# The opening of a graph-count build written in another order, with a first group of 256 nodes and keys turned two pairs ahead

## The reference, cut to what matters

```
edge_index = jnp.stack([src, dst])
h = jnp.maximum(_layernorm(x, axis=-1), 0.0)
x = x + _L0_gnn_ref(h, edge_index, ...)
h = jnp.maximum(_layernorm(x, axis=-1), 0.0)
x = x + _L1_gnn_ref(h, edge_index, ...)
```

## Time and profile before

| what | value |
|---|---|
| median of 3 runs | 963.67 us (963.1 to 963.69) |
| the profiled execution's own time | 960.25 us |
| its span | 958.0 us |
| end of `build` on PE | 398.04 us |
| PE busy | 883.7 us |
| DVE busy | 716.7 us |
| ACT busy | 496.7 us |
| POOL busy | 345.8 us |

### The profile page before, as it was taken

The page is one execution under the profiler, slowest core; times in us unless marked ns, Lnnn a source line. Parts: engine busy times, 40 slices in busy tenths (PEclk is TensorE's granted clock), DMA queues, the critical chain, the costliest instruction groups (busy, mean ns, idle before and its releaser), DMA issues.

```text
span 958.0 us, 25402 instructions
## 1 busy us (share of the span) xinstructions
PE 883.7 (92%) x11397; PEld 740.0 (77%) x11397; DVE 716.7 (75%) x679; ACT 496.7 (52%) x534; POOL 345.8 (36%) x255
## 2 busy tenths in 40 slices
PE   0589999999999979989999999999999989999995
PEld 0368888889989969867888887778888867777774
DVE  6879999999999979295667656665656566777672
ACT  2655555464645534264443454443444467777772
POOL 5775674638471640112567645471000000000000
PEclk9999999999999989999999999999999999999998
DMA  3024334433443333415333434434342357777761
GB/s 108 18 80 148 109 120 145 149 126 102 145 149 129 107 117 111 139 40 154 117 115 116 121 111 118 131 116 129 105 116 75 114 174 238 240 238 242 255 196 38
DMA packets 81377, 126.87 MB, mean 132 GB/s; under 512 B 9808, under 2 KB 58064, under 8 KB 81136
## 3 DMA queue, kind: packets, MB, share of 16 engines
q1 hardware_dynamic: 78128, 121.98, 40.8%
q0 software_dynamic: 3136, 3.22, 1.5%
HBM read 84.22 MB, written 40.94 MB: 131 GB/s over the span
## 4 chain that ended last, share of the span: by engine, by line
PE 50%; DVE 5%; issue 2%; ACT 1%; POOL 0%; DVEq 0%; ACTq 0%
PE net_ps_hi L1164 14%; PE net_ps_hi L1147 13%; PE net_ps_lo L1147 13%; PE net_ps_mt L1090 5%; PE net_ps_ft L1090 3%; DVE hT L849 1%; DVE hT L844 1%; PE net_ps_mt L1199 1%; ACT net_wide L1002 1%; DVE net_wide L752 1%; DVE net_first L856 1%; PE net_ps_mt L1194 1%; DVE net_h_parts L920 0%; DVE hT L909 0%; POOL net_wide L798 0%
## 5 line engine op out<-in xcount | busy, mean ns | idle before, releaser
L1002 ACT ACTIVATE net_wide<-net_raw 128x3584 fp32r<-128x3584 uint8 (+1 forms) x77 | 232.6, 3020 | 37.3 <-PE net_ps_hi L1164 25.5
L752 DVE CAST net_wide<-net_raw 128x3584 fp32r<-128x3584 uint8 (+1 forms) x103 | 202.7, 1974 | 65.2 <-PE net_ps_lo L1147 45.1
L1147 PE MATMUL net_ps_hi<-net_wide,net_first 128*128 128x512 f32 (+1 forms) x637 | 248.2, 393 | 0.1
L461 ACT ACTIVATE build_cnts<-build_ps_cnt 128x980 uint16<-128x980 f32 (+4 forms) x176 | 154.3, 901 | 167.1 <-PE build_ps_cnt L551 161.9
L1147 PE MATMUL net_ps_lo<-net_wide,net_first 128*128 128x512 f32 (+1 forms) x637 | 240.6, 381 | 0.0
L571 PE MATMUL build_ps_out<-build_parts_pad,build_cnts 128*128 128x195 bf16 x2401 | 225.4, 250 | 1.0 <-issue 0.9
L342 DVE TENSOR_TENSOR build_hot_lo<-build_grid_lo,build_keys_t 128x4096 bf16<-128x4096 bf16 x100 | 224.6, 2284 | 0.0
L571 PEld LDWEIGHTS build_ps_out<-build_parts_pad,build_cnts 128*128 128x128 fp8e4 x2401 | 205.6, 98 | 5.2 <-issue 1.8
L1164 PE MATMUL net_ps_hi<-net_wide,net_second 128*128 128x512 f32 (+1 forms) x637 | 156.7, 398 | 2.9 <-DVE net_second L934 2.4
L254 POOL DMA_INDIRECT build_edges<-in_edges,build_start_i x49 | 120.6, 2462 | 100.9 <-DVE build_start_i L326 73.6
L1164 PEld LDWEIGHTS net_ps_hi<-net_wide,net_second 128*128 128x128 f32 x637 | 115.5, 190 | 39.2 <-ACT net_wide L1002 9.7
(11 more groups left out here) (158 smaller groups left out, 670.3 us busy)
## 6 DMA issues: line engine op xcount, KB each, us to landing
net_raw<-edge_counts SPq DMA_DIRECT2D x168, 448.0 KB, 3.6
edge_counts<-build_cnts SPq DMA_DIRECT2D x168, 224.0 KB
xres<-in_x SPq DMA_DIRECT2D x1, 1568.0 KB, 7.3
net_raw<-edge_counts SPq DMA_DIRECT2D x14, 112.0 KB, 2.0
out<-xres SPq DMA_DIRECT2D x12, 128.0 KB, 4.2
build_rows<-in_dst_rows,build_row_i POOLq DMA_INDIRECT x49, 3.2
build_edges<-in_edges,build_start_i POOLq DMA_INDIRECT x49, 2.9
edge_counts<-build_cnts SPq DMA_DIRECT2D x7, 112.0 KB
```

Source lines behind the costliest of these rows:

```text
L461: nc.scalar.activation(pairs[u % A_RING][:, 0:n, :, d.start // 2:d.stop // 2], ps_cnt[b % CNT_RING][:, 0:n, 0:len(d) // 2 * NW].rearrange( ...
L752: return issue(expanded[e % WIDE_RING][:, 0:n, :, :].rearrange("p w a d -> p (w a d)"), raw[e % RAW_RING][:, 0:n, :, :].rearrange("p w a d ...
L1002: expand(act, lambda to, x: nc.scalar.activation(to, x, ACT.Identity), e).then_inc(grown["act"], 1)
L1147: last = nc.tensor.matmul(ps[(b + 1) % 2][:, 0:n * P], first[:, c, lo:lo + H], expanded[e % WIDE_RING][:, 0:n, k, :], start=(c == 0), stop ...
```

## The change

**Groups.** `SPANS` becomes 0-2, 2-6, 6-10, 10-18, 18-26, 26-34, 34-42 and 42-49: still eight groups, with a third one of four windows (256 nodes a pair) and a last one of seven. `FIRST_PAIR` is now 0, 1, 3, 5, 9, 13, 17, 21.

**Keys.** The short count step is now the sixth (`SHORT = 5`), and there PE turns the keys of pair `u + 2` instead of `u + 1` (`u` from 1 on). The keys of pairs 1 and 2 are turned together in the opening.

**Lookups.** POOL issues them one after another without waiting for `counted`; DVE finds starts and keys at places given by `starts_at` and `keys_at`, ACT compares at `compare_step`.

**Remainders.** `take_first` leaves `h64` minus the first part in PSUM; `take_second` subtracts the second part onto it with one more matmul, so the second full-precision product is gone. ACT's roundings of one seventh follow each other closely.

**Order.** DVE finds the first starts after two of four centrings, and ACT loads its table by a one-column `Sign` before the first rows land. In pair 1 each third of `use(0)` stands ahead of the count steps, not behind.

```diff
-SHORT = 2
+SHORT = 5
-PACE = 3, 2
-SPANS = [(0, 2), (2, 6)] + [(w, min(w + 2 * STEP, NW)) for w in range(6, NW, 2 * STEP)]
+SPANS = [(0, 2), (2, 6), (6, 10)] + [(w, min(w + 2 * STEP, NW)) for w in range(10, NW, 2 * STEP)]
+def compare_step(g):
+    return {3: (1, 3), 4: (5, 0)}.get(g, (FIRST_PAIR[g] - 5, 3))
+def starts_at(g):
+    return {3: (3, 0), 4: (6, 1)}.get(g, (FIRST_PAIR[g] - 3, 0))
+def keys_at(g):
+    return {2: (1, 1), 3: (4, 3)}.get(g, (FIRST_PAIR[g] - 1, 0))
...
                 gather_rows(0, *SPANS[0])
-                gather_rows(1, *SPANS[1])
+                gather_rows(1, SPANS[1][0], SPANS[1][1] - 1)
                 gather_edges(0, *SPANS[0])
+                gather_rows(1, SPANS[1][1] - 1, SPANS[1][1])
+                gather_rows(2, *SPANS[2])
+                gather_edges(1, *SPANS[1])
...
+                for g in range(2, len(SPANS)):
+                    gather_edges(g, *SPANS[g])
+                    if g + 1 < len(SPANS):
+                        gather_rows(g + 1, *SPANS[g + 1])
...
-                    if k == turn_step(u) and u + 1 < NU:
-                        turn_keys(u + 1, b % CNT_RING)
+                    if k == SHORT and 0 < u < NU - 2:
+                        turn_keys(u + 2, ps_key[b % CNT_RING])
...
+                def take_first(q):
+                    pe.wait_ge(part0, q + 1)
                     if q >= 2:
-                        pe.wait_ge(part1, q - 1)
+                        pe.wait_ge(part2, q - 1)
+                    nc.tensor.matmul(left_over(q), ident[:, :], h64[:, sevenths[q], :], start=True, stop=False)
+                    nc.tensor.matmul(left_over(q), minus_b[:, :], parts64[:, sevenths[q], 0, 0:F], start=False, stop=True).then_inc(rest, 1)
+                def take_second(q):
+                    pe.wait_ge(part1, q + 1)
+                    nc.tensor.matmul(left_over(q), minus_b[:, :], parts64[:, sevenths[q], 1, 0:F], start=False, stop=True,
+                                     skip_group_check=True).then_inc(rest2, 1)
...
+                        third = 2 * (NW + 1) * i // len(TURNS), 2 * (NW + 1) * (i + 1) // len(TURNS)
+                        if u == 1:
+                            use(0, *third)
                         for k in range(lo, hi):
                             count(u, k)
-                        use(u - 1, 2 * (NW + 1) * i // len(TURNS), 2 * (NW + 1) * (i + 1) // len(TURNS))
+                        if u > 1:
+                            use(u - 1, *third)
```

More of the change, by code:

```diff
@@ L586, in _ @@
                 pe.wait_ge(consts, 9)
-                turn_keys(0, 2).then_inc(first_turned, 1)
-                def take_off(q, w, parts, last):
-                    nc.tensor.matmul(left_over(q), ident[:, :], h64[:, w, :], start=True, stop=False)
-                    for t in range(parts):
-                        ins = nc.tensor.matmul(left_over(q), minus_b[:, :], parts64[:, w, t, 0:F], start=False, stop=(t == parts - 1))
-                    ins.then_inc(last, 1)
-                for k in range(4):
-                    count(0, k)
@@ L613, in _ @@
-                for k in range(6, steps(0)):
-                    count(0, k)
+                        pe.wait_ge(part2, q - 1)
+                    nc.tensor.matmul(left_over(q), ident[:, :], h64[:, sevenths[q], :], start=True, stop=False)
[4 more added lines that the diff above has]
+                                     skip_group_check=True).then_inc(rest2, 1)
@@ new lines, in count_first @@
+                def count_first(lo, hi):
+                    for k in range(lo, hi):
+                        count(0, k)
+                count_first(0, 2)
+                take_first(0)
+                take_first(1)
+                take_second(0)
+                take_second(1)
+                take_first(2)
+                take_first(3)
+                count_first(2, 4)
+                take_second(2)
+                take_second(3)
+                take_first(4)
+                take_first(5)
```

151 lines of the change are left out of this document (73 added, 78 removed).

## The result

The change made the kernel slower: **992.45 us** (median of 4 runs, 989.09 to 993.51) against 963.38 (960.96 to 963.69) beside it, a ratio of **1.030** (95% interval 1.027 to 1.033). I had forecast 965.0 with a range of 955 to 970, so the time lies 22 us outside it.

What follows compares the result with a forecast made beforehand. PE (busy 92%) and DVE nearly full in the middle of `build`, DVE setting the pace, PE the tail. Opening gains went into later waits: `build` 399.3 for 398.04, 960.25 + 1.3 = 961.5 profiled, 965.0 us median, range 955 to 970.

Steps and rivals of the forecast that it cites:

- Opening order: Opening of `build`: ACT's one chain has keys of pair 1 copied at 50.8, so pair 1 gains only 0.9 us.
- First group of 256 nodes: After pair 1: pair 2 starts at 64.7, pair 3 at 76.9, 4.6 us ahead, of which 0.9 is key work put off.
- Lookups: Group 3: starts at 83.0, eight lookups take 20.3 us, edges at 105.2, a new DVE wait of 2.9 us.
- The last group: End of `build`: last lookups held at POOL's block end as before; stall 5.9 us (bounds 0 and 10.5), keys ready at 324.8.
- Keys turned two pairs ahead: From pair 3: DVE's short waits (4.2 us) go; PE stands 14.6 us from 93.1; pair 8 at 150.7, pair 20 at 310.6.
- rival A: Last group: unpaced lookups land in time, stall of 5.9 and low clock's 2.0 go; `build` 391.4, 957.1 us; chance 0.24.
- The sum: End of `build`: 324.8 + 72.5 + 2.0 = 399.3, 1.3 us later than 398.04; median 965.0; chance 0.48.
- D: Turn in pair 3: a held group 3 lookup adds up to 10 us, 975; or all last seven held, 969.6; chance 0.13.
- B: Lookups: not slowed by DVE's compares, eight take 10 us, the 2.9 at group 3 goes too; 954.2 us; chance 0.04.
- C: Opening: ACT's chain is shorter, keys of pair 1 at 47, all behind shifts about 3.8 us; 961.2 us; chance 0.11.

Runs made afterwards that it cites:

- e3: The kernel before with POOL's waits for count steps taken away and nothing else: 951.13 us on chip 1; the same kernel on chip 3 took 964.47 us.
- e13: The changed kernel with one tiny DVE memset behind each `hot_lo` from pair 2 on, on chip 1: 953.96 us.
- e12: The changed kernel as it is, run as a control on chip 1: 992.41 us.
- e6: The changed kernel with the starts of groups 3 and 5 to 7 half a pair of comparisons earlier, on chip 2: 995.34 us.
- e8: The kernel before with lookups unpaced and, of the change, only the first group of 256 nodes with its tables, on chip 2: 979.18 us.
- e5: The changed kernel with one tiny DVE memset behind each `hot_lo` from pair 2 on, on chip 2: 993.87 us.
- e11: The changed kernel with groups of nodes and places of starts and keys as before, keys still two pairs ahead, on chip 3: 986.48 us.
- e14: The kernel before, lookups still paced, with only the tiny memset behind each comparison of lanes, on chip 1: 952.21 us, ratio 0.990.
- e17: The changed kernel with the tiny memset and keys turned one pair ahead instead of two, on chip 4: 960.86 us, ratio 0.999 to the kernel before.

## Why the prediction was wrong

**Opening order** and **First group of 256 nodes** were near. Pair 1 started at 52.72 (predicted 50.8, a wait of 6.94 for its keys instead of 5.2), pair 3 at 78.81 (76.9), starts of group 3 at 84.89 (83.0).

**Lookups** is the step that failed. It took the 20.3 us that eight lookups had needed in the middle before, and had the edges landed at 105.2. Measured were 12.76 + 6.77 us for the first two and edges at 114.3. The step priced only the quick form of the lookup and not its second form, of which the trace had two examples. And it carried the 20.3 us over from groups where DVE had waited for turned keys 7 us earlier to groups where, by the prediction's own next step, it would not.

**The last group** failed for the same reason: I called the block's end the one thing that sets its two held lookups apart, and so confined them there. e3 has that end and no hold, the changed kernel has holds in three groups without it. The other thing that set them apart was DVE's wait ahead of the lookups. Without the memset the 12 us form came wherever DVE had worked on without a wait for 24 us or more, and not elsewhere. It cost a stall of 8.04 at group 7, for the 5.9 in the sum, and 9.30 and 9.36 at groups 5 and 6, for which the sum had zero.

**Keys turned two pairs ahead** was half right. It said that DVE's short waits for turned keys go, and they went, but it booked that as harmless: with them went what had kept lookups of groups 3 to 6 quick. The turn itself was right in mechanism. PE stood at pair 3, 19.0 us for 14.6: it came there at 97.9 (predicted 93.1), and the keys, late by group 3's hold, let it go on at 116.9 (107.7). Where holds are taken away the step's numbers come out. e13 has a new wait of 2.23 at `find_keys` (2.9), `hot_a` of pair 5 at 108.59 (109.5), pair 8 at 149.53 (150.7), pair 20 at 312.07 (310.6). Its `build` ends at 391.97, where rival A (the last lookups in time) had 391.4, and it takes 953.96 for A's 957.1.

**The sum.** In the changed kernel `build` ended at 429.67, 30.4 us behind the 399.3 of the sum. Taking the holds away gave 36.8 (e12 against e13), of which the sum had 7.9 in its last group (5.9 of stall, 2.0 of low clock). That leaves 28.9 of the 30.4 for the holds; the keys of pair 1 were 1.9 late. Two slips in the working change nothing: the sum's own range is 960.0 to 968.5 by its bounds, not 961 to 969, and from 319.20 to 344.72 it is 25.5 us.

**The rivals.** D had the mechanism, held lookups of group 3 reaching PE through the turn, and gave it +10 at one place (975) or the last group (969.6), with a chance of 0.13. It happened at three turns and at the last group, where the block's end had nothing to do with it, as far as the runs show, and D never summed it over them: 10 at each of groups 3, 5 and 6 and 4.6 at the last would have been 965.0 + 34.6 = 999.6. B, no slowing by compares, is out: in every run the usual lookup beside the long comparisons took about 1.9 us or more. C had too early an opening. A's quick last lookups came in e3, e6, e8 and the kernels with the memset.

**What the Trainium skill says of it.** Every trace here shows lookups tied to DVE's comparisons, 0.94 us alone and 1.9 beside them, and 12 of the 13 without a memset some of 12 us. The Trainium skill ("SBUF — State Buffer", SBUF: two separate sides, and Who interferes with whom) has a DVE instruction with two SBUF inputs contend with a GpSimd instruction that reads SBUF, the pair of ports they share being taken for the whole instruction, and it calls `tensor_reduce` free of it on this chip. The rows agree with the comparison as the holder and with the reduce letting a lookup through (its end at 98.07, after the reduce of 97.17). They differ on the length: 12.76 us spans five instructions, not one. And its statement that tensor_tensor did not stall such transfers, which I weighed in the prediction, does not hold for these lookups.

## What stays open

Why a recent wait of DVE, or a memset, lets a lookup through at the next boundary between two comparisons is not known, and the wait alone was not tried. Shown is that with a memset none was held, in six kernels on four chips, and that without it a hold stood in 12 of 13 traces. No other tiny instruction was tried, so what about the memset does it is open too. Nor do I know why PE's signal is late on chips 2 and 3 under bursts of lookups; I saw it in e5, e6 and e8 to e11 and in no run on chips 1 or 4, and it was not taken apart. Whether e5's and e13's difference is the chip rests on one execution of each. The result looks like chip 1 (963.38 and 992.45), and its trace of the changed kernel has no late signal; that of the kernel before has one wait of ACT of 3.47 us that looks like it, at 74.57. e14 was not run on chips 2 or 3.

## What to carry to other kernels

Two odd rows in a trace are a price list, not an accident: ask what the sum becomes if every instruction of that kind takes the rare form, and at how many places it would reach the path. Then compare the odd rows with the ordinary ones in what came before them, and not only beside them: DVE's wait of a few tenths of a microsecond, 7 us earlier, told them apart here, and over all 65 groups such a wait came with a quick lookup and its absence with a held one. Where a change takes an engine's short waits away, look at who was living in them, here the indirect lookups of POOL. A tiny memset behind each `hot_lo` gave 38.5 us in the new kernel and 9.7 in the old. And judge an order (one or two pairs ahead) only after such a hold is gone, since it turned the sign of that comparison.

## What the hardware showed that I had not expected

- An indirect lookup of 0.94 us took up to 12.76 us beside back-to-back comparisons, ending 0.35 us after the next `tensor_reduce`, and never over 4.02 us (e17) with a memset of 0.06 us behind each `hot_lo`.
- Without the memset, the 26 held groups were asked for 24.3 to 59.7 us after VectorE's last wait, the 39 others 0.4 to 8.7 us after one.
- The same program differed by 13 us between chips (951.13 and 964.47), and the same edit by 40 (953.96 and 993.87), while the kernel before lay between 957.47 and 962.78.
- On two chips ACT had the signal of a finished count only 7 to 11 us after its last matmul started, while POOL issued lookups back to back.
